# A decoder's latent attention loop: keys turned by a transposing transfer instead of TensorE, rows rotated by VectorE two batches ahead, contexts formed a batch later

## The chip, the cores and the metric

The kernel runs on one core of one Trainium2 chip. The metric is the device time of one execution in microseconds (us), taken as the median of several runs. TensorE (PE) multiplies matrices, VectorE (DVE) and ScalarE (ACT) work on rows of SBUF and PSUM, GpSimd (POOL) does a part of the elementwise work, and SyncE (SP) issues the transfers that 16 DMA engines carry out.

## The reference, cut to what matters

The whole program is a two-layer decoder on x of shape (32, 56, 256): in each layer a self attention, a cross attention to a context, and a mixture of experts. The change is in the cross attention of layer 0, the latent attention. Its context is (32, 1500, 64): 32 batches of 1500 rows of 64 numbers.

```python
kv_rope = kv_c * cos[None] + _rotate_half(kv_c) * sin[None]      # (32, 1500, 64)
q_r = jnp.einsum('bshq,hqr->bhsr', q_big, W_qr)
k_r = jnp.einsum('bld,hdr->bhlr', kv_rope, W_kr)
scores = jnp.einsum('bhsr,bhlr->bhsl', q_r, k_r)
attn = jax.nn.softmax(scores, axis=-1)
ctx_c = jnp.einsum('bhsl,bld->bhsd', attn, kv_rope)
```

The rotated rows serve twice: turned (64 on partitions, rows along the free axis) as keys for the scores, and as they are as values for the contexts.

## The kernel before

The latent attention (function `latent_attention`) first makes the queries of all 32 batches (`QT`), multiplied with the products of all weights, so that the scores of one batch are one product of 16 heads x 56 queries against 1500 rows. Then comes the loop over the 32 batches, the subject of the change. Every engine has an order written out by hand in its own `body(b, par)`; `over_tiles` runs the first two batches unrolled, the middle ones two by two in a hardware loop and the last ones unrolled, and `par` is the buffer, b mod 2. Semaphores alone tie the engines.

One batch has 1500 rows as 12 tiles (KT) of 125 rows (KP). Its work:

- SP loads the rows of the batch after (`lat_raw`, L2454), copies the queries of a batch into both halves of the partitions (`lat_Q`, four transfers, L2471), and takes the denominators of two batches back through DRAM: `spread_reciprocals` sends `lat_den` to 128 partitions (L2482), waits for the reciprocals, stores them (L2486) and loads them spread over the partitions (`lat_rD`, L2493).
- POOL rotates the rows in fp32 with four operations on 125x768 or 125x384 (L2520, L2522, L2525, L2528), ACT rounds them to fp16 (`high`, L2696), and POOL subtracts that from the exact rows to get the low halves (L2534). High and low halves lie side by side in `kk`. ACT also copies the rotated rows to `kv` (L2702).
- PE turns `kk`: 12 tiles, each in two halves of 64 columns, in two portions of 8 and 4 tiles (`turn`, L2582), into PSUM bank 7; ACT copies each portion to `kT` (`evacuate`, L2687). Each batch has a portion of 8 tiles, done a batch ahead, and one of 4.
- PE computes the scores in three groups `g` of four units (L2617; a unit is 8 heads x 2 tiles, three terms of high and low halves), ACT takes the exponential of each unit (L2739) into `Pb`, which has 8 slots. The ring of score banks holds three units, so the fourth unit of a group waits for the exponential of the first.
- After the scores of a group PE multiplies four tiles of `Pb` with `kv` (`values`, L2595, fp32). The last four tiles of a batch come in group 0 of the next.
- DVE sums the 12 tiles of `Pb` in 11 additions (`lat_dsum`, L2819 and L2824), each dependent on the one before. After these sums are complete PE multiplies them with ones (`denominators`, L2605, group 0 of the next batch). ACT copies the context (L2708) and the denominators (L2714) out of PSUM, DVE takes reciprocals (L2805, after the addition of tile 6) and multiplies context and reciprocals (`context`, L2809, after the addition of tile 10).

The lines that make POOL wait for a free buffer, and PE for the low halves:

```python
                        if past(b, 2):
                            pool.wait_ge(kT_done, (b - 1) * NTURN)
                        nc.gpsimd.tensor_tensor(halves(par, True), paired(rot[:, par]),
                                                halves(par, False), ALU.subtract).then_inc(kl_made, 1)
```

## Time and profile before

| | us |
|---|---|
| median of 3 runs | 1811.01 |
| lowest and highest of the 3 | 1799.75, 1813.59 |
| the profiled execution | 1797.95 |
| its span | 1796.2 |
| the loop over batches in it, first scores to last denominators | 354.4 to 961.6 |
| one batch in the steady part of the loop | 18.73 |

| engine | busy us | share of the span |
|---|---|---|
| PE | 1431.9 | 80% |
| DVE | 1361.9 | 76% |
| ACT | 1053.4 | 59% |
| POOL | 652.1 | 36% |

The profiled execution is quicker than the median of the three timed runs by 13 us. The loop is a third of the span. Busy shares over the whole span mix stages with different limits; what matters for the change are the stretches inside the loop.

### The profile page before, as it was taken

To read this page: it belongs to the slowest core of one execution; us is meant where nothing else is said; L and a number is where in the kernel's file an instruction comes from. 1 tells how busy PE (TensorE), PEld (TensorE's weight loads), DVE (VectorE), ACT (ScalarE), POOL (GpSimd) and SP (SyncE) were. 2 spreads that over 40 slices of the span, in tenths; PEclk is the share of its full clock that TensorE was granted. 3 is DMA by queue.
4 is the path that set the end of the run, shared out by engine and by line. 5 is a ranking of instruction groups with operands and counts; after the bars stand their busy time and mean duration, and the time that the engine had idled before them with its cause. 6 is when DMAs were issued, how large, how long until landed. Compare 5 with 4: busy or idle time off the path is not lost. (4 is left out here: it accounts for less than half of the span.)

```text
span 1796.2 us, 40092 instructions
## 1 busy us (share of the span) xinstructions
PE 1431.9 (80%) x13869; PEld 917.4 (51%) x13884; DVE 1361.9 (76%) x2397; ACT 1053.4 (59%) x1795; POOL 652.1 (36%) x658
## 2 busy tenths in 40 slices
PE   1687776899999999999997754992778699945992
PEld 0455553444444444444444743991566567634891
DVE  6888875699988888889886784547898656576774
ACT  1767763577677777777773243551676555454461
POOL 1212213165455465554630145562333200037241
PEclk9856665999999999999998857996899989968996
DMA  6950000111221212222110225444000000034335
GB/s 138 315 165 1 1 1 35 38 36 49 61 59 49 72 48 60 60 48 72 48 45 7 60 74 161 157 148 128 1 1 0 1 2 1 1 96 141 107 102 164
DMA packets 106444, 123.65 MB, mean 69 GB/s; under 512 B 23553, under 2 KB 87625, under 8 KB 106211
## 3 DMA queue, kind: packets, MB, share of 16 engines
q1 hardware_dynamic: 96451, 98.87, 20.5%
q0 software_dynamic: 7776, 21.28, 3.2%
q10 hardware_dynamic: 2112, 2.10, 0.4%
q8 instruction: 66, 1.08, 0.3%
q14 instruction: 39, 0.32, 0.1%
HBM read 66.85 MB, written 40.30 MB: 60 GB/s over the span
## 5 line engine op out<-in xcount | busy, mean ns | idle before, releaser
L2824 DVE TENSOR_TENSOR lat_dsum<-lat_dsum,lat_Pb 125x896 f32<-125x896 f32 x320 | 477.3, 1492 | 67.4 <-ACT lat_Pb L2739 58.5
L2739 ACT ACTIVATE lat_Pb<-banks 125x896 f32<-125x896 f32 x384 | 329.0, 927 | 141.2 <-PE banks L2617 114.8
L2595 PE MATMUL banks<-lat_Pb,lat_kv 125*64 125x448 f32 x1536 | 306.4, 541 | 0.0
L2617 PE MATMUL banks<-lat_Q,lat_kT 64*125 64x448 f16 x2304 | 258.8, 360 | 4.2 <-DVE lat_QT L2785 1.3
L2617 PEld LDWEIGHTS banks<-lat_Q,lat_kT 64*125 64x125 f16 x2304 | 142.6, 134 | 149.3 <-issue 66.9
L2595 PEld LDWEIGHTS banks<-lat_Pb,lat_kv 125*64 125x64 f32 x1536 | 100.6, 137 | 146.4 <-issue 137.6
L2534 POOL TENSOR_TENSOR lat_kk<-lat_rot,lat_kk 125x768 f16<-125x768 f32 x32 | 65.8, 2057 | 279.3 <-ACT lat_kk L2696 279.3
L3165 POOL DMA_INDIRECT sent_outputs<-moe_yb,moe_yidx x98 | 95.6, 975 | 115.5 <-ACT moe_yb L3424 100.5
L3303 PE MATMUL banks<-moe_w2d,moe_gT 88*128 (+3 forms) x780 | 100.0, 278 | 17.6 <-DVE moe_gT L3642 13.7
L3630 DVE COPY moe_xTb<-banks 128x1024 f16<-128x1024 f16 x49 | 33.9, 691 | 76.8 <-PE banks L3270 76.8
L3303 PEld LDWEIGHTS banks<-moe_w2d,moe_gT 88*128 88x128 f16 (+1 forms) x780 | 75.5, 99 | 30.1 <-issue 19.7
L3157 POOL DMA_INDIRECT sent_rows<-moe_arena,moe_idx x64 | 71.2, 1112 | 52.5 <-DVE moe_idx L3571 33.5
L2528 POOL TENSOR_TENSOR lat_rot<-lat_rot 125x768 f32<-125x768 f32 x32 | 80.1, 2502 | 2.5
L3220 PE MATMUL banks<-moe_xTb,moe_w2i 128*88 128x256 f16 (+1 forms) x588 | 73.2, 275 | 0.0
L2520 POOL TENSOR_TENSOR lat_rot<-lat_raw,lat_cosK 125x768 f32<-125x768 f32 x32 | 67.4, 2106 | 14.9 <-POOL lat_kk L2534 9.1
L1471 POOL TENSOR_TENSOR bit_vv<-bit_vf,bit_one 128x256 f16<-128x256 f32 x16 | 11.6, 727 | 164.0 <-PE banks L1758 153.5
L3220 PEld LDWEIGHTS banks<-moe_xTb,moe_w2i 128*88 (+1 forms) x588 | 62.7, 112 | 3.3
L3383 ACT ACTIVATE moe_gT<-banks 88x512 f32<-88x512 f32 x37 | 21.9, 592 | 60.9 <-PE banks L3220 60.9
L3270 PE MATMUL banks<-id,moe_xb 128*128 128x128 f16 x392 | 30.7, 223 | 33.1 <-DMA moe_xb<-sent_rows 33.1
L2522 POOL TENSOR_TENSOR lat_rot<-lat_raw,lat_sinK 125x384 f32<-125x384 f32 x32 | 54.7, 1709 | 2.5
L2525 POOL TENSOR_TENSOR lat_rot<-lat_raw,lat_sinK 125x384 f32<-125x384 f32 x32 | 53.8, 1680 | 2.5
L2687 ACT ACTIVATE lat_kT<-banks 128x1000 f16<-128x1000 f16 x64 | 52.7, 823 | 0.0
(450 smaller groups left out, 3111.8 us busy)
## 6 DMA issues: line engine op xcount, KB each, us to landing
lat_Q<-lat_QT SPq DMA_DIRECT2D x128, 112.0 KB, 3.4
moe_xb<-sent_rows SPq DMA_DIRECT2D x49, 257.0 KB
lat_raw<-in_ctx_dram SPq DMA_DIRECT2D x32, 375.0 KB
sent_rows<-zero SPq DMA_DIRECT2D x1, 7453.0 KB, 39.8
lat_rD<-lat_reciprocals SPq DMA_DIRECT2D x62, 112.0 KB, 2.8
moe_arena<-sent_outputs SPq DMA_DIRECT2D x12, 512.0 KB, 7.5
sent_rows<-zero SPq DMA_DIRECT2D x1, 5140.0 KB, 57.6
sent_outputs<-zero SPq DMA_DIRECT2D x1, 4096.0 KB, 41.6
```

The lines of the kernel that those rows point to most:

```text
L2520: s(nc.gpsimd.tensor_tensor(rot[:, par], r, cosK[:], ALU.mult))
L2522: s(nc.gpsimd.tensor_tensor(rot2[:, :, 0:Q], r[:, :, Q:DC], sinK[:, :, 0:Q], ALU.mult))
L2528: nc.gpsimd.tensor_tensor(rot[:, par], rot[:, par], rot2[:], ALU.add).then_inc(rotated, 1)
L2534: nc.gpsimd.tensor_tensor(halves(par, True), paired(rot[:, par]), halves(par, False), ALU.subtract).then_inc(kl_made, 1)
L2595: ins = nc.tensor.matmul(ps[u * DC:(u + 1) * DC, 6, 0:8 * T], kv[:, par, tt, :], Pb[:, tile_slot(tt, par), u, :], start=tt == 0, stop=tt = ...
L2617: ins = nc.tensor.matmul(ps[0:KP, n % 3 * 2 + q, 0:8 * T], kT[rows, par, 2 * pair + low, 0:KP], Q2[rows, par, w, 8 * u:8 * u + 8, :].rearr ...
L2739: nc.scalar.activation(Pb[:, slot:slot + 2, u, :], ps[0:KP, n % 3 * 2:n % 3 * 2 + 2, 0:8 * T], ACT.Exp, scale=1.0 / QSCALE).then_inc(exp_d ...
L2824: ins = nc.vector.tensor_tensor(dsum[:, par], dsum[:, par], Pb[:, tile_slot(tt, par)], ALU.add)
L3157: nc.gpsimd.indirect_dma_start(xg[:, :], bass.IndirectOffsetOnAxis(ap=idx[:, c, i:i + 1], axis=0), rows[:, i, :], None).then_inc((sent0, s ...
L3165: nc.gpsimd.indirect_dma_start(ytok[:, :], bass.IndirectOffsetOnAxis(ap=yidx[:, n, h:h + 1], axis=0), yb[:, n % 3, h, :], None).then_inc(y ...
L3220: ins = nc.tensor.matmul(ps[0:FP, dst, j * BN:(j + 1) * BN], w[:, u, c, j * FP:(j + 1) * FP], rhs(v, c), start=a + c == 0, stop=a == 2 and ...
L3303: ins = nc.tensor.matmul(dst, gT2[:, n % 2, u, j, h * P:(h + 1) * P], w[:, v, j, :], start=a + j == 0, stop=last and not (gated and b < 0))
```

## The change

What it does, engine by engine:

- **TensorE** no longer turns the keys (24 small matmuls a batch fewer, no `turn`), and **ScalarE** no longer copies them out of PSUM (two activations fewer a batch). `high` of the batch after comes after the third exponential instead of the fourth.
- **SyncE** issues one transposing transfer a batch, `kk` (128 partitions x 12 x 128 fp16, 384 KB) to `kT`, after the low halves of that batch are made. It stands between the copies of the queries and `spread_reciprocals`. PE waits for its landing (`kT_in`) at group 0.
- **GpSimd** rotates the first two batches alone and does nothing in the loop.
- **VectorE** rotates the rows of batch b + 2 after the addition of tile 8 of batch b (four operations), subtracts the low halves of batch b + 1 after tile 2, takes the reciprocals after tile 7 instead of 6, and multiplies the context of batch b - 2 after tile 1, where it multiplied that of b - 1 after tile 10. The copied context has two buffers.
- `kk` is given three more partitions' worth of rows (125 to 128), set to zero once by GpSimd ahead of the loop (32 partitions), and rows of `kT` are 128 long instead of 126. `good` shares the buffer of `den`.

```diff
-            kk = sb("kk", [KP, 2, KT, 2 * DC], F16, c=main)
+            kk = sb("kk", [P, 2, KT, 2 * DC], F16, c=main)
...
-            rD, pv = sb("rD", [P, 8 * T], c=main), sb("pv", [P, 8 * T], c=main)
+            rD, pv = sb("rD", [P, 8 * T], c=main), sb("pv", [P, 2, 8 * T], c=main)
...
+                        sp.wait_ge(kl_made, b + 1)
+                        sp.sem_inc(turn_begun, 1)
+                        sp.dma_start(kT[:, par], kk[:, par].rearrange("p t d -> p (t d)"),
+                                     transpose=True).then_inc(kT_in, 16)
                         if past(b, 2):
                             spread_reciprocals(b - 2)
...
+                    nc.gpsimd.memset(kk[96:P], 0.0).then_inc(rests_zeroed, 1)
...
-                    def turn(b, par, c):
...
-                        for tt in range(8 * c, min(8 * c + 8, KT)):
-                            n = tt - 8 * c
-                            for q in range(2):
-                                rows = slice(q * DC, (q + 1) * DC)
-                                ins = nc.tensor.transpose(
-                                    bank[rows, n * KS:n * KS + KP],
-                                    kk[:, par, tt, rows], id16[0:KP, 0:KP])
-                        ins.then_inc(kT_done, 1)
...
                             if g == 0:
-                                pe.wait_ge(kT_made, b * NTURN + 1)
+                                pe.wait_ge(kT_in, 16 * b + 16)
                                 pe.wait_ge(spread[par], 4 * half_count(b, par))
-                            if g == 2:
-                                pe.wait_ge(kT_made, b * NTURN + 2)
                             for pair in (2 * g, 2 * g + 1):
                                 for u in range(2):
                                     scores(b, par, pair, u)
-                            if g == 0:
-                                turn(b, par, 1)
-                            if g == 2 and live(b + 1, B):
-                                turn(b + 1, (par + 1) % 2, 0)
...
                         if past(b, 2):
-                            act.wait_ge(kT_done, (b - 1) * NTURN)
+                            act.wait_ge(kT_in, 16 * (b - 1))
...
-                            if n == 3:
-                                evacuate(b, par, 1)
-                                if live(b + 1, B):
-                                    high(b + 1, (par + 1) % 2)
+                            if n == 2 and live(b + 1, B):
+                                high(b + 1, (par + 1) % 2)
...
+                    def kept_context(b, par):
+                        dve.wait_ge(pv_kept, b + 1)
+                        dve.wait_ge(rec_in, 32 * b + 32)
+                        context(b, pv[:, par])
+
+                    def rotated_rows(b, par):
+                        r = raw[:, par]
+                        dve.wait_ge(raw_in[par], half_count(b, par))
+                        dve.wait_ge(rotated, b)
+                        dve.wait_ge(kv_made, b - 1)
+                        dve.wait_ge(kl_made, b - 1)
+                        nc.vector.tensor_tensor(rot[:, par], r, cosK[:], ALU.mult
+                                                ).then_inc(products_made, 1)
+                        nc.vector.tensor_tensor(rot2[:, :, 0:Q], r[:, :, Q:DC], sinK[:, :, 0:Q],
+                                                ALU.mult).then_inc(products_made, 1)
+                        nc.vector.tensor_tensor(rot2[:, :, Q:DC], r[:, :, 0:Q], sinK[:, :, Q:DC],
+                                                ALU.mult).then_inc(products_made, 1)
+                        dve.wait_ge(products_made, 3 * b - 3)
+                        nc.vector.tensor_tensor(rot[:, par], rot[:, par], rot2[:], ALU.add
+                                                ).then_inc(rotated, 1)
+
+                    def low(b, par):
+                        dve.wait_ge(kh_made, b + 1)
+                        nc.vector.tensor_tensor(halves(par, True), paired(rot[:, par]),
+                                                halves(par, False), ALU.subtract).then_inc(kl_made, 1)
...
-                            if tt == 6 and past(b, 1):
+                            if tt == 1 and past(b, 2):
+                                kept_context(b - 2, par)
+                            if tt == 2 and past(b, 1) and live(b + 1, B):
+                                low(b + 1, other)
+                            if tt == 7 and past(b, 1):
                                 reciprocals(b - 1)
-                            if tt == KT - 2 and past(b, 1):
-                                dve.wait_ge(pv_kept, b)
-                                dve.wait_ge(rec_in, 32 * b)
-                                context(b - 1, pv[:])
-
-                    over_tiles(dve, body, 0, n=B)
+                            if tt == 8 and live(b + 2, B):
+                                rotated_rows(b + 2, par)
+
+                    over_tiles(dve, body, 1, n=B)
+                    kept_context(B - 2, 0)
```

**SyncE, one batch of the hardware loop.** Before: the queries of the batch, then the denominators and reciprocals of two batches back (ISA and REGISTER_ALU rows work out wait values and addresses).

```order
L2471 DMA lat_Q<-lat_QT 64x2x448
L2471 ISA
L2471 DMA lat_Q<-lat_QT 64x2x448 x3
L2482 DMA lat_den<-lat_den 64x1x7 x2
L2486 ISA
L2486 DMA lat_reciprocals<-lat_rec 128x7
L2489 ISA
L2493 DMA lat_rD<-lat_reciprocals 64x448 x2
```

The same place now:

```order
L2472 DMA lat_Q<-lat_QT 64x2x448
L2472 ISA
L2472 DMA lat_Q<-lat_QT 64x2x448 x3
L2478 DMA_TRANSPOSE lat_kT<-lat_kk 128x12x128
L2487 DMA lat_den<-lat_den 64x1x7 x2
L2491 ISA
L2491 DMA lat_reciprocals<-lat_rec 128x7
L2494 ISA
L2498 DMA lat_rD<-lat_reciprocals 64x448 x2
```

One instruction is new, and the transfers of the denominators, and all behind them, stand behind it and its wait.

**VectorE, the middle of one batch of the hardware loop**, from the reciprocals on. Before:

```order
L2805 RECIPROCAL lat_rec<-lat_den 128x7
L2823 REGISTER_ALU
L2824 TENSOR_TENSOR lat_dsum<-lat_dsum,lat_Pb 125x896
L2814 REGISTER_ALU
L2823 REGISTER_ALU
L2824 TENSOR_TENSOR lat_dsum<-lat_dsum,lat_Pb 125x896
```

Now, with L2760 the reciprocals, L2808 the additions, L2778 to L2785 the rotation of batch b + 2:

```order
L2760 RECIPROCAL lat_rec<-lat_den 128x7
L2798 REGISTER_ALU
L2807 REGISTER_ALU
L2808 TENSOR_TENSOR lat_dsum<-lat_dsum,lat_Pb 125x896
L2774 ISA
L2778 TENSOR_TENSOR lat_rot<-lat_raw,lat_cosK 125x768
L2780 TENSOR_TENSOR lat_rot<-lat_raw,lat_sinK 125x12x32
L2782 TENSOR_TENSOR lat_rot<-lat_raw,lat_sinK 125x12x32
L2784 ISA
L2785 TENSOR_TENSOR lat_rot<-lat_rot 125x768
L2807 REGISTER_ALU
L2808 TENSOR_TENSOR lat_dsum<-lat_dsum,lat_Pb 125x896
```

The four operations of the rotation stand between the additions of tiles 8 and 9, and the beginning of the next batch has the other two that moved:

```order
L2803 TENSOR_TENSOR lat_dsum<-lat_Pb 125x896
L2764 ISA
L2764 TENSOR_TENSOR lat_QT<-lat_pv,lat_rD 128x448
L2798 REGISTER_ALU
L2807 ISA
L2808 TENSOR_TENSOR lat_dsum<-lat_dsum,lat_Pb 125x896
L2789 REGISTER_ALU
L2790 TENSOR_TENSOR lat_kk<-lat_rot,lat_kk 125x6x128
```

There the context (L2764) follows the first addition and the low halves (L2790) the second.

## Rows read from the trace of the kernel before

**Rows 1.** Busy time by stretch: steady loop, stretch, PE, PEld, DVE, ACT, POOL, clock, DMA

```profile
602.99:960.70 357.71, 356.66 (x2816) 161.31 (x2816) 308.33 (x254) 260.68 (x339) 175.95 (x86) 1.00 0.22 54
```

**Rows 2.** Timeline of PE, one batch: start us, us, engine, line, operation

```profile
602.99 2.73 PE L2617 MATMUL banks<-lat_Q,lat_kT 64*125 64x448 f16 x24
605.65 0.41 PE L2582 MATMUL banks<-id,lat_kk 125*64 125x125 f16 x8
605.90 3.18 PE L2595 MATMUL banks<-lat_Pb,lat_kv 125*64 125x448 f32 x16
608.91 0.92 PE L2605 MATMUL banks<-lat_dsum,lat_ones 125*64 125x448 f32 x4
609.75 2.73 PE L2617 MATMUL banks<-lat_Q,lat_kT 64*125 64x448 f16 x24
612.41 3.23 PE L2595 MATMUL banks<-lat_Pb,lat_kv 125*64 125x448 f32 x16
615.57 2.65 PE L2617 MATMUL banks<-lat_Q,lat_kT 64*125 64x448 f16 x24
618.15 0.63 PE L2582 MATMUL banks<-id,lat_kk 125*64 125x125 f16 x16
618.62 3.18 PE L2595 MATMUL banks<-lat_Pb,lat_kv 125*64 125x448 f32 x16
621.72 0.59 PE L2617 MATMUL banks<-lat_Q,lat_kT 64*125 64x448 f16 x4
```

**Rows 3.** Timeline of ACT: denominators copied, once a batch; two long intervals

```profile
378.81 0.54 ACT L2714 ACTIVATE lat_den<-banks 128x448 f32<-128x448 f32 x1
400.81 0.54 ACT L2714 ACTIVATE lat_den<-banks 128x448 f32<-128x448 f32 x1
...
457.68 0.54 ACT L2714 ACTIVATE lat_den<-banks 128x448 f32<-128x448 f32 x1
480.16 0.54 ACT L2714 ACTIVATE lat_den<-banks 128x448 f32<-128x448 f32 x1
```

**Rows 4.** Timeline in the second long interval: DVE, then PE

```profile
473.11 0.62 DVE L2809 TENSOR_TENSOR lat_QT<-lat_pv,lat_rD 128x448 f32 x1 [1.59 <-DMA lat_rD<-lat_reciprocals]
...
476.32 1.53 PE L2605 MATMUL banks<-lat_dsum,lat_ones 125*64 125x448 f32 x4 [2.38 <-DVE lat_dsum L2824]
```

**Rows 5.** Timeline of DVE in the batch of rows 2

```profile
604.90 0.62 DVE L2809 TENSOR_TENSOR lat_QT<-lat_pv,lat_rD 128x448 f32 x1
605.43 1.08 DVE L2824 TENSOR_TENSOR lat_dsum<-lat_dsum,lat_Pb 125x896 f32<-125x896 f32 x1
606.44 1.08 DVE L2819 TENSOR_TENSOR lat_dsum<-lat_Pb 125x896 f32<-125x896 f32 x1
607.56 2.22 DVE L2824 TENSOR_TENSOR lat_dsum<-lat_dsum,lat_Pb 125x896 f32<-125x896 f32 x2
...
617.80 0.19 DVE L2805 RECIPROCAL lat_rec<-lat_den 128x7 f32 x1
617.91 5.97 DVE L2824 TENSOR_TENSOR lat_dsum<-lat_dsum,lat_Pb 125x896 f32<-125x896 f32 x4
```

**Rows 6.** Line L2824, whole program: ns min/median/max, first and last start

```profile
L2824 DVE TENSOR_TENSOR lat_dsum<-lat_dsum,lat_Pb x320: 1083/1093/2661, 358.6 to 958.6; 125x896 f32<-125x896 f32 x160
```

**Rows 7.** Timeline of ACT in the batch of rows 2: groups 0 and 1

```profile
603.97 3.35 ACT L2739 ACTIVATE lat_Pb<-banks 125x896 f32<-125x896 f32 x4 [1.99 <-DVE lat_dsum L2824]
...
611.97 2.54 ACT L2739 ACTIVATE lat_Pb<-banks 125x896 f32<-125x896 f32 x3
```

**Rows 8.** Timeline of SP's queue in that batch: start us, us of issuing

```profile
602.98 2.81 SPq L2471 DMA_DIRECT2D lat_Q<-lat_QT  x4
612.11 1.16 SPq L2482 DMA_DIRECT2D lat_den<-lat_den  x2
...
620.87 0.32 SPq L2454 DMA_DIRECT2D lat_raw<-in_ctx_dram  x1
```

**Rows 9.** Transfers of lat_den, 440 to 640 us: issue to landing

```profile
DMA to landing us min/median/max: 1.8/1.8/1.9
```

More of the change, by code:

```diff
@@ L24 @@
 MAGIC = 12582912.0
-KS = 126
+KS = 128
 KT, KP = 12, 125
@@ L2390, in halves @@
             def halves(par, low):
-                return kk[:, par, low:KT:2, :]
+                return kk[0:KP, par, low:KT:2, :]
             def paired(a):
@@ L2433, in live_columns @@
                 return not isinstance(g, int) or g + 1 < NG
-            own_pool = sem("pool")
+            own_pool, products_made = sem("pool"), sem("row_products_made")
+            Q = DC // 2
             raw_in = [sem("even_rows_loaded"), sem("odd_rows_loaded")]
-            kv_made, kT_done, kT_made = sem("kv_made"), sem("kT_done"), sem("kT_made")
+            kv_made, kT_in = sem("kv_made"), sem("keys_turned")
             rotated, kh_made, kl_made = sem("rows_rotated"), sem("kh_made"), sem("kl_made")
@@ L2443, in latent_attention @@
                 sem("good_reduced"), sem("good_counted"))
-            NTURN = 2
             def past(i, least=0):
@@ L2510, in _ @@
                     pool.wait_ge(tables, 32)
-                    Q = DC // 2
-                    def body(b, par):
-                        r = raw[:, par]
-                        pool.wait_ge(raw_in[par], half_count(b, par))
-                        if past(b, 2):
-                            pool.wait_ge(kv_made, b - 1)
-                        s(nc.gpsimd.tensor_tensor(rot[:, par], r, cosK[:], ALU.mult))
-                        s.settle()
+                    for b in range(2):
+                        r = raw[:, b]
+                        pool.wait_ge(raw_in[b], 16)
+                        if b:
+                            pool.wait_ge(rotated, 1)
+                        s(nc.gpsimd.tensor_tensor(rot[:, b], r, cosK[:], ALU.mult))
                         s(nc.gpsimd.tensor_tensor(rot2[:, :, 0:Q], r[:, :, Q:DC], sinK[:, :, 0:Q],
                                                   ALU.mult))
-                        s.settle()
                         s(nc.gpsimd.tensor_tensor(rot2[:, :, Q:DC], r[:, :, 0:Q], sinK[:, :, Q:DC],
@@ L2527, in body @@
                         s.settle()
-                        nc.gpsimd.tensor_tensor(rot[:, par], rot[:, par], rot2[:],
-                                                ALU.add).then_inc(rotated, 1)
+                        nc.gpsimd.tensor_tensor(rot[:, b], rot[:, b], rot2[:], ALU.add
+                                                ).then_inc(rotated, 1)
                         pool.wait_ge(rotated, b + 1)
                         pool.wait_ge(kh_made, b + 1)
-                        if past(b, 2):
-                            pool.wait_ge(kT_done, (b - 1) * NTURN)
-                        nc.gpsimd.tensor_tensor(halves(par, True), paired(rot[:, par]),
-                                                halves(par, False), ALU.subtract).then_inc(kl_made, 1)
-                        pool.wait_ge(kl_made, b + 1)
-                    over_tiles(pool, body, 0, s, 3, n=B)
+                        nc.gpsimd.tensor_tensor(halves(b, True), paired(rot[:, b]), halves(b, False),
+                                                ALU.subtract).then_inc(kl_made, 1)
                 @block.tensor
@@ L2601, in denominators @@
                         pe.wait_ge(summed, (b + 1) * (KT - 1))
-                        pe.wait_ge(kT_made, min(b + 1, B - 1) * NTURN + 2 if isinstance(b, int)
-                                   else b * NTURN + (NTURN + 2))
+                        if past(b, 1):
+                            pe.wait_ge(den_kept, b)
                         for u in range(2):
@@ L2629, in body @@
                                 queries_of(g)
-                            turn(0, 0, 0)
                             queries_of(NG - 1)
@@ L2680, in keep_queries @@
                                                  ACT.Copy).then_inc(qh_made, 1)
-                    def evacuate(b, par, c):
-                        n = min(8, KT - 8 * c)
-                        act.wait_ge(kT_done, b * NTURN + (c + 1))
-                        if c == 0 and past(b, 2):
-                            act.wait_ge(s_done, (b - 1) * KT)
-                        nc.scalar.activation(
-                            kT[:, par, 8 * c:8 * c + n, 0:KP],
-                            ps[:, 7, :].bitcast(F16)[:, 0:n * KS].rearrange(
-                                "p (n k) -> p n k", n=n)[:, :, 0:KP], ACT.Copy).then_inc(kT_made, 1)
                     def high(b, par):
@@ L2749, in body @@
                                 keep_denominators(b - 1)
-                            if n == 10 and live(b + 1, B):
-                                evacuate(b + 1, (par + 1) % 2, 0)
                     over_tiles(act, body, 1, n=B)
@@ L2810, in context @@
                                                 source, rD[:], ALU.mult).then_inc(ct_made, 1)
+                    def kept_context(b, par):
[16 more added lines that the diff above has]
+                        nc.vector.tensor_tensor(rot[:, par], rot[:, par], rot2[:], ALU.add
+                                                ).then_inc(rotated, 1)
+                    def low(b, par):
+                        dve.wait_ge(kh_made, b + 1)
+                        nc.vector.tensor_tensor(halves(par, True), paired(rot[:, par]),
+                                                halves(par, False), ALU.subtract).then_inc(kl_made, 1)
                     def body(b, par):
+                        if not live(b, B):
+                            return
+                        other = (par + 1) % 2
                         for tt in range(1, KT):
```

24 lines of the change are left out of this document (9 added, 15 removed).

## The prediction

> **What bounds the kernel now.** I first asked for the busy times of the steady part of the loop. TensorE is busy for 356.66 of 357.71 us at full granted clock, VectorE for 308, ScalarE for 261, GpSimd for 176 [rows 1]. A busy PE can still hide waits in the length of its rows, so the timeline of one batch came next [rows 2]: scores start at 602.99 and, a batch later, at 621.72, which is 18.73 us for a batch. In between stand three groups, each of scores and then values. The group in the middle, which has nothing else, takes 2.66 us from its scores to its values (609.75 to 612.41) and 5.82 in all. The turned keys stand in the two others: in the first, values start 2.91 us after the scores, in the third 3.05.
>
> The beginning of the loop is not steady. Denominators are copied once a batch, and two of the intervals are 22.00 and 22.48 us in place of 18.73 [rows 3]. In the second of them VectorE waits 1.59 us for the reciprocals spread by a transfer, and then TensorE waits 2.38 us for VectorE's sum [rows 4]; the row of TensorE is also longer than its like (1.53 against 0.92 [rows 2, 4]).
>
> VectorE has two speeds. An addition lasts 1.08 to 1.12 us in most rows, but four of them take 5.97, 1.49 each [rows 5, 6]. Two facts on its pace: a row followed by an independent one costs less than its duration (the context of 0.62 starts 0.53 before the next, an addition of 1.08 starts 1.01 before), while an addition that waits for the one before costs 1.12 [rows 5].
>
> **The change part by part.**
>
> Turned keys off TensorE. The portion of 4 tiles costs from 605.65 to 605.90, 0.25 us; the portion of 8 from 618.15 to 618.62, 0.47 us [rows 2]. Nothing on TensorE overlaps them, so both are on the path: 0.72 us a batch, a batch of 18.01 us, 31 x 0.72 = 22.3 us in all. The groups then start at 0, 6.51 and 12.33 us of a batch.
>
> Two activations off ScalarE, and the rounding to high halves one unit earlier. ScalarE isn't the bound; what counts is the first exponential of a group, since the fourth unit of scores waits for it. It starts 0.98 us into the group and lasts 0.92 with a pitch of 0.81 (four take 3.35, three 2.54) [rows 7]. The rounding, taken as long as an exponential, then stands before the fourth exponential, which ends at 3.52 + 0.81 + 0.81 = 5.1 us; the first unit of group 1 that needs that exponential's bank comes after 6.5. I cost it at nothing. If it were late, it would add at most its own 0.8 us.
>
> GpSimd out of the loop. The four-in-a-row additions at 1.49 would fall to 1.12. VectorE gets five operations a batch that are new to it. Their durations here come from its own rows: 448 elements take 0.62 and 896 take 1.08 [rows 5], so 1.03 ns an element and 0.16 fixed; 768 elements make 0.95, 384 make 0.56. At 0.08 less for an independent follower, the rotation costs 0.87 + 0.48 + 0.48 + 0.87, and 0.1 for the wait for the products: 2.8 us. The low halves cost 0.87. The sum of VectorE for a batch: 5 additions at 1.01 and 6 at 1.12, 11.8; context 0.53; reciprocals 0.1; rotation and low halves 3.7; together 16.1 us in 18.0. It fits with 1.9 us to spare, but in a fixed order, so the places matter. Walking through a batch: tile 8 can be added when the second exponential of group 2 ends, 12.33 + 0.98 + 0.92 + 0.81 = 15.0 us. Then come the addition, the rotation and three more additions, to 22.2, which is 4.1 us into the next batch. TensorE wants the complete sum for the denominators at 608.91 - 602.99 - 0.25 = 5.7 us into it [rows 2]. That leaves 1.5 us. Then tile 1, the context, tile 2 (whose exponential is there at 5.1) and the low halves, made at 7.6 us. Caught up by tile 4, which has to wait for its exponential to 9.6. So VectorE is late at one place and idle at another, and never holds TensorE.
>
> The stalls at the beginning. Both parts of the cause go: additions beside GpSimd's operations, and a context that waits for its reciprocals in the batch in which they are made. The new place of the context is a batch later, so the transfer has some 4 us more than it needs. I take both long intervals back to normal: 3.27 + 3.75 = 7.0 us.
>
> The transposing transfer. The trace has none, so its cost T (issue on SP, or the time until the rings are free behind it, whichever is more) has to be bounded. What hangs on it is not mainly the keys: low halves at 7.6 us, keys needed at 18.0, so over 10 us for issue and landing. It is what stands behind it in SP's queue, the transfers of the denominators. Before, these are issued at 612.11, 9.1 us into the batch, for 1.16 us, with 1.8 to land [rows 8, 9]. VectorE's reciprocals wait for that landing, and all of VectorE's batch is queued behind the reciprocals, the next low halves too. That closes a ring: low halves, transfer T, denominators (half of the issue and 1.8 of landing, with 0.2 for semaphores: 2.6 us), reciprocals, tile 8, rotation, tiles 9 to 11, tile 1, context, tile 2, low halves: 0.1 + 1.01 + 2.8 + 1.12 + 1.12 + 1.01 + 1.01 + 0.53 + 1.01 + 0.95 = 10.7 us. The ring takes T + 13.3. Up to T = 4.7 it is shorter than TensorE's 18.01 and costs nothing. At 5.4 all of the gain of the steady loop is gone.
>
> Bounds for T: one transfer is issued in 0.32 us at the least; four copies of queries take 2.81, 0.70 each [rows 8]. Each of these has 128 runs of 448 elements, so 5.5 ns a run; the new transfer has 128 x 12 = 1536 rows of 256 bytes, which at that price take 8.4 us. Counting its 12 blocks as 12 transfers gives 12 x 0.32 = 3.8 at the low price and 8.4 at the high. I keep 0.3 and 8.4 as the ends and take 3.8: it is one instruction, as a load is, but cannot be one move. A gain below zero isn't in it.
>
> A rule on this: the Trainium skill, in "DMA: Bandwidth & Descriptors", "Latency and other measured facts", gives 261 GB/s for a transposing transfer on one kernel; for 393,216 bytes that would be an estimated 1.5 us, and the sum would stay as it is. The same page has, for earlier generations, 262,144 cycles of issue for 8,192 tiles, and calls the tile one of 256 bytes in "SDMA does more than copy"; by that reading 1,536 tiles would take an estimated 49,152 cycles, tens of microseconds a batch, and the loop would be more than twice as long. No run here shows either yet; it is a reason not to trust the low end too far.
>
> The rest: zeroing on GpSimd lies ahead of the loop, beside other work; the last context comes after the loop, where VectorE otherwise waits for the last denominators, at most 0.5 us; both at nothing.
>
> **The sum** is 22.3 + 7.0 = 29.3 us. Against the profiled execution, 1797.95, it gives 1769. That execution is 13 us quicker than the median of the three runs; against the median, 1811.01, it gives 1782, and that is my forecast, since the result is a median.
>
> **The rivals.**
>
> *The transfer holds the ring* (slower). Decides from T = 5.4 upward. For it: 1536 short rows, and a queue in which everything waits in turn; against it: a single instruction on idle rings. At T = 7 a batch takes 20.3 us, 31 x 1.5 = 48 more, less the 7 of the beginning: 1852. At 8.4 it takes 21.7, and the time is 1896.
>
> *The transfer takes a part*. T between 4.7 and 5.4, a batch of about 18.4: 10 + 7 gained, 1794.
>
> *VectorE becomes the bound*. If the rotation costs double (the halves of 32 columns are strided, and no row shows them on VectorE), 16.1 becomes 18.9 us, and a batch lasts 18.9: 5 lost, 7 gained, 1809.
>
> *TensorE gets its 0.72 us back as waits*, because the fourth unit of scores or the values then wait for exponentials: the turn would have been cover for ScalarE. Against it: the group without a turn has the same 2.66 us [rows 2]. Only the 7 us stay: 1804.
>
> **How the numbers follow.** Chances: the forecast 0.52, the transfer as the bound 0.22, a part 0.12, waits instead 0.08, VectorE 0.06. A kernel like this can be told from no change from about 1% on, 18 us, so below 1793 is faster and above 1829 slower. Faster: the forecast and a third of the partial case, 0.55. Slower: the transfer above T = 6.1 and a rest for the other cases, 0.20. Within 1%: 0.25. The range: 1764 is 5 below the sum against the profiled execution, for waits that I haven't counted; 1855 is the transfer at T = 7.1. What is left out, mostly a T above that, is 0.15.
>
> **What would show it.** Values 2.6 us after scores in all three groups; the interval between two copies of denominators 18.0 from the second batch on; every addition 1.09; rotation rows of 0.95 and 0.56; on SP a transposing row of under 4.7 us, and the reciprocals not waiting. I am wrong if that row, or the landing of the denominators behind it, is longer; VectorE's reciprocals would then wait each batch, and TensorE before the denominators.

## The result, and the profile after

| | before | changed |
|---|---|---|
| median of 4 runs, us | 1809.5 | 1779.8 |
| lowest and highest | 1799.75, 1813.59 | 1776.0, 1782.12 |
| profiled execution, its span | 1797.95, 1796.2 | 1782.12, 1780.3 |
| mean interval between two copies of denominators | 18.97 | 18.10 |

The ratio of changed to before is 0.9847, with a 95% interval of 0.9811 to 0.9884: 1.5% less time, and clear of the noise. The forecast was 1782.

The copies of the denominators on ScalarE in the changed kernel, the rows that answer to [rows 3]:

```profile
379.91 0.54 ACT L2674 ACTIVATE lat_den<-banks 128x448 f32<-128x448 f32 x1
397.96 0.54 ACT L2674 ACTIVATE lat_den<-banks 128x448 f32<-128x448 f32 x1
416.09 0.54 ACT L2674 ACTIVATE lat_den<-banks 128x448 f32<-128x448 f32 x1
...
887.36 0.54 ACT L2674 ACTIVATE lat_den<-banks 128x448 f32<-128x448 f32 x1
905.17 0.54 ACT L2674 ACTIVATE lat_den<-banks 128x448 f32<-128x448 f32 x1
922.91 0.54 ACT L2674 ACTIVATE lat_den<-banks 128x448 f32<-128x448 f32 x1
```

Read as intervals between their starts, there is no long one any more: 18.05, then 18.13 throughout, and 17.81 and 17.74 for the two last batches, which are written out. TensorE's timeline over one batch, from group 1 to group 0 of the next, against [rows 2]:

```profile
595.55 2.73 PE L2594 MATMUL banks<-lat_Q,lat_kT 64*125 64x448 f16 x24
598.21 3.23 PE L2572 MATMUL banks<-lat_Pb,lat_kv 125*64 125x448 f32 x16
601.37 2.65 PE L2594 MATMUL banks<-lat_Q,lat_kT 64*125 64x448 f16 x24
603.95 3.23 PE L2572 MATMUL banks<-lat_Pb,lat_kv 125*64 125x448 f32 x16
607.11 2.73 PE L2594 MATMUL banks<-lat_Q,lat_kT 64*125 64x448 f16 x24
609.77 3.23 PE L2572 MATMUL banks<-lat_Pb,lat_kv 125*64 125x448 f32 x16
612.83 0.92 PE L2582 MATMUL banks<-lat_dsum,lat_ones 125*64 125x448 f32 x4
613.68 2.73 PE L2594 MATMUL banks<-lat_Q,lat_kT 64*125 64x448 f16 x24
```

Scores to values is 2.66, 2.58 and 2.66 us in the three groups. Values that follow scores directly last 3.16 us to the next scores (603.95 to 607.11); those that followed a turn took 3.10 (618.62 to 621.72 in [rows 2]), and in group 0, to the denominators, 3.06 now and 3.01 before. VectorE in the same stretch, with L2808 the additions, L2790 the low halves, L2778 to L2785 the rotation:

```profile
594.59 1.08 DVE L2808 TENSOR_TENSOR lat_dsum<-lat_dsum,lat_Pb 125x896 f32<-125x896 f32 x1
595.59 0.95 DVE L2790 TENSOR_TENSOR lat_kk<-lat_rot,lat_kk 125x768 f16<-125x768 f32 x1
596.46 1.08 DVE L2808 TENSOR_TENSOR lat_dsum<-lat_dsum,lat_Pb 125x896 f32<-125x896 f32 x1
598.81 4.47 DVE L2808 TENSOR_TENSOR lat_dsum<-lat_dsum,lat_Pb 125x896 f32<-125x896 f32 x4 [1.27 <-ACT lat_Pb L2698]
603.20 0.19 DVE L2760 RECIPROCAL lat_rec<-lat_den 128x7 f32 x1
604.12 1.09 DVE L2808 TENSOR_TENSOR lat_dsum<-lat_dsum,lat_Pb 125x896 f32<-125x896 f32 x1 [0.72 <-ACT lat_Pb L2698]
605.12 0.95 DVE L2778 TENSOR_TENSOR lat_rot<-lat_raw,lat_cosK 125x768 f32<-125x768 f32 x1
605.99 0.55 DVE L2780 TENSOR_TENSOR lat_rot<-lat_raw,lat_sinK 125x384 f32<-125x384 f32 x1
606.46 0.55 DVE L2782 TENSOR_TENSOR lat_rot<-lat_raw,lat_sinK 125x384 f32<-125x384 f32 x1
607.05 0.96 DVE L2785 TENSOR_TENSOR lat_rot<-lat_rot 125x768 f32<-125x768 f32 x1
607.92 3.33 DVE L2808 TENSOR_TENSOR lat_dsum<-lat_dsum,lat_Pb 125x896 f32<-125x896 f32 x3
```

Additions that follow each other have a pitch of 1.12 (4.47 for four), and VectorE is idle at two places a batch, 1.27 and 0.72 us, both times until an exponential is done. SP's queue there, against [rows 8]:

```profile
596.63 1.49 SPq L2478 DMA_TRANSPOSE lat_kT<-lat_kk  x1
598.16 1.51 SPq L2487 DMA_DIRECT2D lat_den<-lat_den  x2
603.52 0.38 SPq L2491 DMA_DIRECT2D lat_reciprocals<-lat_rec  x1
```

The transposing transfer is issued in 1.49 us. Its time from the start of issue to landing, over the stretch from 440 to 900 us:

```profile
DMA to landing us min/median/max: 3.7/3.7/3.7
```

**Where the time went.** Between the first and the last copy of denominators lie 569.24 us before and 543.00 now, 26.2 less. Of these, the beginning gives 7.9 (its four intervals of 22.00, 19.40, 22.48 and 18.98 less four of 18.73) and 30 intervals of 0.61 less give 18.3. The medians are 29.7 apart. The two profiled executions are only 15.8 apart: behind the last copy of denominators the changed one needed 857.4 us and the one before 848.1, in code that is the same, apart from the last context. In the 150 us from 438 us behind the loop's end, for instance, the granted clock was 0.87 against 0.94. That is a difference between two executions. No run separates it from the change, and I don't ascribe it to the change: in the second measurement of the changed kernel, beside the one before, the medians are 25.6 us apart, close to the 26.2 of the loop.

### The profile page after: what moved, and what is told of

Its sections match the earlier page's. It is cut to its first block and busy times, and to the rows that moved or that the text cites. A ratio compares the mean times of both kernels' runs of the same rounds, so it can differ in the third digit from the quotient of the medians.

```text
span 1780.3 us, 38229 instructions
## 1 busy us (share of the span) xinstructions
PE 1423.0 (80%) x13101; PEld 909.2 (51%) x13116; DVE 1342.5 (75%) x2547; ACT 1009.8 (57%) x1731; POOL 349.8 (20%) x509
## 5 line engine op out<-in xcount | busy, mean ns | idle before, releaser
L2808 DVE TENSOR_TENSOR lat_dsum<-lat_dsum,lat_Pb 125x896 f32<-125x896 f32 x320 | 349.5, 1092 | 70.1 <-ACT lat_Pb L2698 62.5
L3290 PEld LDWEIGHTS banks<-moe_w2d,moe_gT 88*128 88x128 f16 (+1 forms) x780 | 77.0, 101 | 30.9 <-issue 19.2
L3386 ACT ACTIVATE moe_uT<-banks,moe_bug 128x256 f32<-128x256 f32 x56 | 23.5, 471 | 49.7 <-PE banks L3207 44.9
L2870 PE MATMUL banks<-lat_B,lat_C 128*56 128x256 f16 x768 | 43.9, 279 | 8.3 <-DVE lat_C L2898 8.3
L2558 PE MATMUL banks<-lat_cols,lat_A 128*128 (+1 forms) x192 | 40.3, 361 | 9.5 <-DVE lat_cols L2726 9.5
L2870 PEld LDWEIGHTS banks<-lat_B,lat_C 128*56 128x56 f16 x768 | 43.4, 110 | 8.5 <-issue 8.3
L3629 DVE TENSOR_TENSOR moe_gT<-moe_gT 88x512 f16<-88x512 f32 (+1 forms) x65 | 44.6, 688 | 3.9 <-ACT moe_gT L3374 2.9
L1131 DVE TENSOR_REDUCE causal_mx<-banks 128x16 f32<-128x896 f32 x16 | 17.5, 1092 | 37.5 <-PE banks L853 37.5
```

The lines of the kernel that those rows point to most:

```text
L2558: ins = nc.tensor.matmul(ps[:, j % 4, 0:GN], A16[:, w, c, 2 * j:2 * j + 2, :].rearrange("p h d -> p (h d)"), cols[:, v, c, ds(g * GN, GN)] ...
L2808: ins = nc.vector.tensor_tensor(dsum[:, par], dsum[:, par], Pb[:, tile_slot(tt, par)], ALU.add)
L2870: ins = nc.tensor.matmul(ps[u * HALF:u * HALF + T, s4 % 2, 0:D], C16[:, s4, low, u, j * T:(j + 1) * T], B16[:, j, wlow, :], start=j == 0 a ...
L3290: ins = nc.tensor.matmul(dst, gT2[:, n % 2, u, j, h * P:(h + 1) * P], w[:, v, j, :], start=a + j == 0, stop=last and not (gated and b < 0))
L3629: nc.vector.tensor_tensor(gT2[:, n % 2, 1], gT[:, n % 2], gT2[:, n % 2, 0], ALU.subtract).then_inc(gl_made, 1)
```

## The experiments

Ten more measurements were made, each of one kernel beside the kernel before on the same chip. The kernel before has medians from 1809.5 to 1828.8 us in these groups, up to 19 us apart, so the ratios count, and the interval between copies of denominators in each trace. That interval hardly varies: the changed kernel has the same 18.10 in the traces of both of its measurements.

| kernel | ratio to before (95%) | mean interval, us | steady interval, us |
|---|---|---|---|
| changed | 0.9847 (0.9811 to 0.9884) | 18.10 | 18.13 |
| turns kept beside the transfer | 0.9967 (0.9946 to 0.9988) | 18.71 | 18.73 |
| rotation alone | 0.9960 (0.9938 to 0.9982) | 18.71 | 18.73 |
| transfer alone | 1.0043 (1.0023 to 1.0064) | 19.10 | 18.13, with long ones |
| transfer twice | 1.0020 (1.0003 to 1.0037) | 19.09 | 19.03 to 19.13 |
| context early | 0.9873 (0.9826 to 0.9920) | 18.10 | 18.13 |
| a value tile between the scores | 0.9898 (0.9863 to 0.9933) | 18.35 | 18.35 |
| transfer and late context | 0.9933 (0.9902 to 0.9964) | 18.50 | 18.47 to 18.72 |
| low halves later | 1.0053 (1.0034 to 1.0073) | 19.22 | 19.25 |
| all batches written out | 0.9789 (0.9741 to 0.9836) | 17.74 | 17.74 |
| changed, again | 0.9849 (0.9801 to 0.9896) | 18.10 | 18.13 |

**Was it TensorE's time?** The changed kernel with transposes of a constant tile at the old places; nobody reads them:

```diff
+                        for tt in range(8 * c, min(8 * c + 8, KT)):
...
+                                nc.tensor.transpose(bank[rows, n * KS:n * KS + KP],
+                                                    id16[0:KP, rows], id16[0:KP, 0:KP])
...
+                            if g == 0:
+                                stand_in(1)
+                            if g == 2 and live(b + 1, B):
+                                if past(b, 1):
+                                    pe.wait_ge(den_kept, b)
+                                stand_in(0)
```

> The changed kernel, with TensorE issuing the same 24 small transposes a batch at the old places (8 after the scores of group 0, 16 after those of group 2), of a constant tile into bank 7, where nobody reads them; the keys still come by the transfer. Theory (the 0.72 us a batch were TensorE's time): the interval between copies of denominators goes from 18.13 back by 0.7 to 18.8 us, the time to about 1780 + 22 = 1802. Rival (TensorE was waiting for something else, and the turns only filled that wait): the interval stays at 18.1 to 18.3 and the time below 1786.

The interval is 18.73, the very one of before, and the ratio loses 0.012 of the changed kernel's gain of 0.015. TensorE's timeline of this kernel has the turns' pitch of 0.25 and 0.47 us again:

```profile
610.02 2.65 PE L2605 MATMUL banks<-lat_Q,lat_kT 64*125 64x448 f16 x24
612.60 0.63 PE L2572 MATMUL banks<-id 125*64 125x125 f16 x16
613.07 3.18 PE L2583 MATMUL banks<-lat_Pb,lat_kv 125*64 125x448 f32 x16
616.17 2.73 PE L2605 MATMUL banks<-lat_Q,lat_kT 64*125 64x448 f16 x24
618.83 0.41 PE L2572 MATMUL banks<-id 125*64 125x125 f16 x8
619.08 3.18 PE L2583 MATMUL banks<-lat_Pb,lat_kv 125*64 125x448 f32 x16
```

These transposes wait for no keys, and their cost is the same. So the turns were TensorE's own time, without any cover, and the rest of the change does nothing for the steady interval while they are there.

**The rotation alone.** The changed kernel with `turn` and `evacuate` back and no transfer:

```diff
-                        sp.wait_ge(kl_made, b + 1)
-                        sp.sem_inc(turn_begun, 1)
-                        sp.dma_start(kT[:, par], kk[:, par].rearrange("p t d -> p (t d)"),
-                                     transpose=True).then_inc(kT_in, 16)
...
+                            if g == 0:
+                                turn(b, par, 1)
+                            if g == 2 and live(b + 1, B):
+                                turn(b + 1, (par + 1) % 2, 0)
```

> The changed kernel without the transposing transfer: TensorE turns the keys and ScalarE copies them out as before, while VectorE rotates the rows, the low halves are early and the contexts a batch later. Theory (the rotation's part of the change is worth only the two long intervals at the loop's start): steady interval 18.7 to 18.85 us, no interval over 19 at the start, time about 1810 - 7 = 1803. Rival (moving the rotation off GpSimd speeds up each batch): steady interval 18.4 or less, time 1795 or less.

The steady interval is 18.73, the first 18.66, and none is long. It gains 0.4%, the stalls of the beginning, and nothing else. This kernel has ScalarE's two copies of the turned keys again, which the one with constant transposes lacks, at the same 18.73: they cost the loop nothing.

**The transfer alone.** The kernel before, with the transfer for the turns; GpSimd and the contexts as they were:

```diff
+                        sp.wait_ge(kl_made, b + 1)
+                        sp.sem_inc(turn_begun, 1)
+                        sp.dma_start(kT[:, par], kk[:, par].rearrange("p t d -> p (t d)"),
+                                     transpose=True).then_inc(kT_in, 16)
...
-                            pool.wait_ge(kT_done, (b - 1) * NTURN)
+                            pool.wait_ge(kT_in, 16 * (b - 1))
```

> The kernel before with the transposing transfer in place of the turns, and nothing else of the change: GpSimd rotates in every batch, the contexts are where they were. Theory: the steady interval falls to 18.1 us as in the changed kernel, but the long intervals at the start stay, so 1810 - 19 to - 22, about 1790. Rival (with additions slowed beside GpSimd VectorE can't keep 18.1 us, so the rotation had to move for the transfer to pay): steady interval 18.4 or more, or new waits of TensorE for VectorE's sum; time 1797 or more.

The rival held. Most intervals are 18.13 as in the theory, but every second to fifth one is 20.5 to 22.3, through the whole loop, and the sum is slower than before. From the waits from 440 to 900 us (engine, what, for whom: us in total, times, longest):

```profile
ACT lat_Pb L2709 <- DVE lat_dsum L2791: 24.7, 11, 2.5
PEld banks L2593 <- DVE lat_dsum L2791: 23.5, 13, 3.3
DVE lat_QT L2776 <- DMA lat_rD<-lat_reciprocals: 19.5, 19, 1.8
```

VectorE waits for the spread reciprocals (the last row) and is late; TensorE (second row) waits for its complete sum before the denominators, and ScalarE (first row) for an addition that frees a slot of `Pb`.

**Which part of the rest heals that?** First the late context added to the transfer, with GpSimd still rotating:

```diff
-                            if tt == KT - 2 and past(b, 1):
-                                dve.wait_ge(pv_kept, b)
-                                dve.wait_ge(rec_in, 32 * b)
-                                context(b - 1, pv[:])
...
+                            if tt == 1 and past(b, 2):
+                                kept_context(b - 2, par)
```

> The kernel before with the transposing transfer and the contexts a batch later in two buffers; GpSimd still rotates all batches. With the transfer alone half of the intervals were 18.13 us, and every few batches one of 20.5 to 22.3 came, where VectorE had waited for the spread reciprocals. Theory (the additions slowed beside GpSimd make the stalls; the late reciprocals are their consequence): most of the long intervals stay, mean interval 18.6 or more. Rival (the wait of the context was the cause): the long intervals are gone, mean interval 18.3 or less, and the rotation need not have moved.

Between the two: the long intervals are gone, so it took the wait of the context to make them, against my theory; but 18.5 is left in place of 18.13, and the ratio is 0.9933, a gain, where the transfer alone was a loss. The busy times of two batches (stretch, PE, PEld, DVE, ACT, POOL, clock, DMA), and VectorE's groups from 440 to 900 us (count, busy us, mean ns), show what then bounds it:

```profile
564.92:601.90 36.98, 36.56 (x250) 15.57 (x248) 36.43 (x27) 24.93 (x32) 21.11 (x11) 1.00 0.44 80
```

```profile
L2796 DVE TENSOR_TENSOR lat_dsum<-lat_dsum,lat_Pb 125x896 f32<-125x896 f32 x248 | 378.8, 1527 | 6.8
L2791 DVE TENSOR_TENSOR lat_dsum<-lat_Pb 125x896 f32<-125x896 f32 x25 | 63.3, 2532 | 0.0
```

VectorE is busy for 36.43 of 36.98 us. Its additions take 1.53 us in the mean and the first of a batch, which lies beside GpSimd's low halves, 2.53, where 1.09 is the pace of the changed kernel. The mean hides two kinds of addition. The kernel before has them too, and there the row of four additions of 5.97 us [rows 5] comes apart into one of 2.59, which lies across GpSimd's last sum, and three of 1.09 behind it:

```profile
617.01 2.54 POOL L2528 TENSOR_TENSOR lat_rot<-lat_rot 125x768 f32<-125x768 f32 x1
617.91 2.59 DVE L2824 TENSOR_TENSOR lat_dsum<-lat_dsum,lat_Pb 125x896 f32<-125x896 f32 x1
620.54 1.09 DVE L2824 TENSOR_TENSOR lat_dsum<-lat_dsum,lat_Pb 125x896 f32<-125x896 f32 x1
```

An addition that meets no operation of GpSimd takes 1.09 in both kernels. The rotation and low halves on GpSimd so cost VectorE 10 x 0.44 + 1.4 = 5.8 us a batch in this kernel; done by VectorE itself, their rows come to 3.96. Then the context put back in the changed kernel:

```diff
-                            if tt == 1 and past(b, 2):
-                                kept_context(b - 2, par)
...
+                            if tt == KT - 2 and past(b, 1):
+                                kept_context(b - 1, other)
```

> The changed kernel with the context of batch b - 1 after the addition of tile 10 of batch b, as before the change (its two buffers stay). The reciprocals are spread by a transfer issued at about 605.0 to 606.1 of the changed trace and landing 2.8 later, 608.9; the addition of tile 10 ends near 610.2. Theory (with the rotation off GpSimd the old place would do): no waits of VectorE for that transfer, interval 18.13, time within 3 us of the changed kernel. Rival (the later context is what keeps VectorE on time): it waits for the transfer, the interval rises above 18.3.

As the theory says: 18.13 in every interval of the hardware loop and no wait for the transfer. The late context is needed only as long as VectorE is slowed; in the changed kernel it brings nothing that these runs could measure.

**The ring over SP and VectorE.** The transfer twice, one after the other:

```diff
-                        sp.dma_start(kT[:, par], kk[:, par].rearrange("p t d -> p (t d)"),
-                                     transpose=True).then_inc(kT_in, 16)
+                        for n in range(2):
+                            if n:
+                                sp.wait_ge(kT_in, 32 * b + 16 * n)
+                                sp.sem_inc(turn_begun, 1)
+                            sp.dma_start(kT[:, par], kk[:, par].rearrange("p t d -> p (t d)"),
+                                         transpose=True).then_inc(kT_in, 16)
```

> The changed kernel with the transposing transfer done twice a batch, the second after the first has landed, so that the transfers of the denominators stand behind 3.7 + 1.5 = 5.3 us in place of 1.5. Theory of the ring (low halves, transfer, denominators, reciprocals, rotation, sums, low halves; 10.7 us of VectorE and 3.3 of the denominators with their measured issue of 1.51 and landing of 2.3): it takes 5.3 + 14.0 = 19.3 us, the interval rises from 18.13 to 19.2 to 19.5, and VectorE's reciprocals wait each batch; time about 1780 + 36 = 1816. Rival (the queue has slack for it, as only the keys' landing counts, which would be at 7.6 + 7.5 = 15 of 18 us): interval and time unchanged.

The interval is 19.1, just under the 19.2 to 19.5 expected, and the wait is where the ring has it. VectorE, from one low halves' row to the next reciprocals, and the queue:

```profile
614.30 0.95 DVE L2794 TENSOR_TENSOR lat_kk<-lat_rot,lat_kk 125x768 f16<-125x768 f32 x1
615.17 5.59 DVE L2812 TENSOR_TENSOR lat_dsum<-lat_dsum,lat_Pb 125x896 f32<-125x896 f32 x5
623.57 0.20 DVE L2764 RECIPROCAL lat_rec<-lat_den 128x7 f32 x1 [2.81 <-DMA lat_den<-lat_den]
...
615.35 5.23 SPq L2482 DMA_TRANSPOSE lat_kT<-lat_kk  x2
620.63 1.48 SPq L2491 DMA_DIRECT2D lat_den<-lat_den  x2
```

From the low halves' end (615.25) to the reciprocals it is 8.3 us: 5.4 until the issue of the denominators begins and 2.9 from there to the reciprocals. And the low halves three additions later:

```diff
-                            if tt == 2 and past(b, 1) and live(b + 1, B):
+                            if tt == 5 and past(b, 1) and live(b + 1, B):
```

> The changed kernel with the low halves after the addition of tile 5 instead of tile 2. By the ring of the prediction with the measured transfer: 14.0 + 1.5 us plus three more additions, 3.3, makes 18.8 to 18.9 against TensorE's 18.13, so the interval rises to 18.8 to 19.0 and the reciprocals wait; time about 22 us over the changed kernel. Rival (the denominators' transfers have slack): interval stays at 18.13.

The interval is 19.25, over the 18.8 to 19.0 expected. Its reciprocals wait 2.5 us a batch, and inside the ring VectorE also waits 0.55 for an exponential between tiles 3 and 4, which the expectation had left out:

```profile
613.36 2.22 DVE L2808 TENSOR_TENSOR lat_dsum<-lat_dsum,lat_Pb 125x896 f32<-125x896 f32 x2 [0.55 <-ACT lat_Pb L2698]
...
621.04 0.20 DVE L2760 RECIPROCAL lat_rec<-lat_den 128x7 f32 x1 [2.48 <-DMA lat_den<-lat_den]
```

The two measure the ring of the changed kernel: 19.1 - (5.3 - 1.5) = 15.3, and 19.25 - 3 x 1.12 - 0.55 = 15.3. Its parts add up to nearly the same, 15.2: 1.6 us from the end of the low halves to the issue of the denominators (596.54 to 598.16 in the changed kernel), 2.9 to the reciprocals, and the 10.7 of VectorE that the prediction added up. The ring has 2.8 us to spare under 18.13. So the early place of the low halves is a necessary part: three additions later the whole change is a loss. By the ring one or two additions later would still cost nothing; that was not tested.

**A value tile between the scores.** An attempt to go further. The fourth unit of scores waits for a free bank, and a tile of values could fill that wait:

```diff
+                            for n in range(4):
+                                if n == 3:
+                                    value_tile(b, par, g, 4 * g - 4)
+                                scores(b, par, 2 * g + n // 2, n % 2)
+                            for tt in range(4 * g - 3, 4 * g):
+                                value_tile(b, par, g, tt)
```

> The changed kernel with the first tile of values of each group put between the third and fourth unit of scores, so that TensorE has 0.75 us of work while the fourth unit's banks are freed. Theory (three waits of some 0.4 us a batch for the exponential of the group's first unit remain in TensorE's time): the interval falls by 3 x 0.4 from 18.13 to 16.9 to 17.2, the ring over SP and VectorE's 16.1 us of work just allow it, and the time is 30 to 37 us under the changed kernel. Rival (switching TensorE between the two kinds of matmul costs as much as it saves, or VectorE's order does not fit): 18.0 or more, no gain.

The rival held: 18.35, slower than the changed kernel's 18.13. One group of that kernel:

```profile
606.98 1.92 PE L2600 MATMUL banks<-lat_Q,lat_kT 64*125 64x448 f16 x18
608.82 0.97 PE L2572 MATMUL banks<-lat_Pb,lat_kv 125*64 125x448 f32 x4
609.73 0.78 PE L2600 MATMUL banks<-lat_Q,lat_kT 64*125 64x448 f16 x6
610.44 2.48 PE L2572 MATMUL banks<-lat_Pb,lat_kv 125*64 125x448 f32 x12
612.84 1.92 PE L2600 MATMUL banks<-lat_Q,lat_kT 64*125 64x448 f16 x18
```

The group takes 5.86 us against 5.74 to 5.82. Scores and values together are 1.84 + 0.71 + 0.91 + 2.40; three tiles at 0.80 would leave 0.80 for the single one and 0.61 for the unit, so each piece of its own costs 0.1 us more. The wait that was there to be saved was 0.1 to 0.2 us a group (2.58 to 2.66 against four units at 0.61), not the 0.4 expected, and the two pieces eat it. Why a separate piece costs more isn't shown.

**All batches written out.** The unrolled last batches had been quicker in both traces:

```diff
-                    over_tiles(pe, body, 1, n=B)
+                    over_tiles(pe, body, 1, n=B, first=B)
```

This is TensorE's line (and the same for SP, ScalarE and VectorE; `over_tiles` then returns before its loop).

> The changed kernel with all 32 batches of the loop written out on each engine, so that waits are for constants and no addresses are worked out. The last two batches, which are written out already, take 17.81 and 17.74 us in place of 18.13, and the groups' first exponential starts 0.82 us in instead of 0.98. Theory (that difference is the cost of the loop form, on the way from scores to exponential): all intervals 17.75 to 17.85, time about 29 x 0.35 = 10 us under the changed kernel beside it. Rival (fetching some thirteen thousand more instructions, or the last batches being quicker only for having no batch after them): intervals stay at 18.1 or show gaps, no gain or a loss.

> The changed kernel once more, beside the one before and the written-out one on the same chip: ratio to the kernel before 0.981 to 0.989 as in the first measurement, interval 18.13.

Written out, every interval is 17.74; the changed kernel beside it has 18.13 and the ratio 0.9849, as in its first measurement. The medians beside each other are 1784.7 and 1795.5: 10.8 us less, for no change of the work; against the kernel before it is 0.9789. TensorE in the kernel written out:

```profile
610.62 2.58 PE L2596 MATMUL banks<-lat_Q,lat_kT 64*125 64x448 f16 x24
613.12 3.23 PE L2574 MATMUL banks<-lat_Pb,lat_kv 125*64 125x448 f32 x16
```

Scores to values is 2.50 instead of 2.66 us; in the trace the difference sits in the time from a group's scores to its first exponential, 0.82 against 0.98. Which part of the loop form makes it (waits against computed values, addresses, the branch) isn't shown.

## Why the prediction was right, and where it wasn't

The time (1782 forecast, 1779.8 measured) and the mechanism of its two terms stand: turned keys, forecast at 22.3 us, gave 18.3 in the loop; the stalls of the beginning, forecast at 7.0, gave 7.9. That the sum of 29.3 us meets the 29.7 between the medians so closely is in part luck: the traces have 26.2 us in the loop, the second measurement has 25.6 between its medians, and the four runs of each kernel spread over 6 and 14 us.

- *Keys off TensorE*: right in mechanism, and the constant transposes show it. The size was 0.72 us a batch by the pitch of the turns' rows; it is 0.61. The term was mis-sized because removing a turn lengthens the values behind it by 0.05 to 0.06 each, as the two timelines show. That is 3.3 us over the loop; the rest is that 31 batches were counted and the traces have 30 intervals.
- *VectorE's work*: durations of 0.95 and 0.56 from a line through two of its rows, measured 0.95 and 0.55; the sum of 16.1 us of 18.0 a batch, measured 254.9 of 290.0 in 16 batches, 15.9. One row was misread: the four additions of 5.97 us are not 1.49 each but one of 2.59 and three of 1.09, and the other three slow ones of that batch (4.87 us for three, at 613.01) are in none of the rows shown. The sum didn't rest on it, since it took 1.01 and 1.12 for all of them. Group times, the late place (the sum done 1.5 us ahead) and the idle place before tile 4 came as walked through.
- *The transfer*: T of 3.8 was taken between 0.3 and 8.4; it is 1.5 us of issue. The 3.8 came from counting 12 blocks as 12 transfers, which no run bears out; the bounds lay on both sides of the threshold, so that the price fell on the right side was not worked out but guessed. The threshold was put at 4.7; from the two experiments it is 1.5 + 2.8 = 4.3, since issue and landing of the denominators came to 2.9 instead of 2.6 and another 0.1 to 0.2 lies between the transfer and them. The ring exists, and the two tries at lengthening it came to 19.1 and 19.25, so the slower rival had the right mechanism and only its price did not occur. Of the two figures that the prediction took from the Trainium skill, "DMA: Bandwidth & Descriptors" ("Latency and other measured facts", and the cycles under "Why a DMA increments its semaphore by 16 and not by 1"), the estimated 1.5 us of moving has room in the trace (3.7 us from issue to landing, with an issue of 1.49), which doesn't show the moving by itself; an issue of tens of microseconds, by the prediction's own count of tiles, is ruled out.
- *GpSimd out of the loop*: here the working was incomplete. The step counted the rotation at VectorE's side as five operations added and otherwise as worth the two long intervals. Alone, with the turns still there, that is what it is worth, 0.4%. But with the transfer in place it is worth more. With neither it nor the late context the transfer loses 0.4%; with the late context alone it gains 0.7%; with the rotation off GpSimd and the context early it gains 1.3%, which is not to be told from the 1.5% of the whole change. So either part turns the loss into a gain, and only the rotation gives the full 18.13. I had slow additions before me [rows 5] and asked only whether the new VectorE fits in 18.0, not whether the old one would have.
- *The stalls of the beginning*: right that both causes went; but the two are not equal. With the transfer in place, faster additions alone take the stalls away; the context's new place alone takes away the long intervals and leaves VectorE full. For the kernel before, without the transfer, the two weren't tried apart.
- *TensorE gets it back as waits*, *VectorE becomes the bound*: neither happened in the changed kernel. VectorE is the bound in the kernel with the transfer, the late context and GpSimd's rotation, though not for the reason of the rival: it is the additions that are slow there.

## What to carry to other kernels

The parts of a change can be worth little or less than nothing one by one (here 0.4% and -0.4%) and more together (1.5%): price each with the others absent, too, and above all ask for every engine whether it could have kept the new pace as it was. When a merged row gives a mean, look at its single instructions before using the mean as a speed. Where a queue carries a transfer that a later step of the same engine waits for, add up the closed ring (steps, issue, landing) and compare it with the bound: it costs nothing until it is longer, and then all of it. And when rows of unrolled and looped copies of the same work stand in one trace, their difference is a first estimate of what the loop form costs: here 18.13 less 17.74 us, and writing everything out gave just that.

## What the runs showed of the hardware that I had not expected

- A transposing transfer of 384 KB from SBUF to SBUF is issued in 1.49 us as one instruction and has landed 3.7 us after its issue began. The two small transfers behind it took 1.51 us to issue, against 1.16 [rows 8], and landed 2.1 us after issue, against 1.8 [rows 9].
- Here GpSimd's elementwise work cost VectorE more than it relieved it of: 5.8 us a batch in slower additions, with the transfer and the late context, against 3.96 for doing the work itself. An addition of 1.09 us took 1.77 across GpSimd's 125x384 products and 2.59 across its 125x768 sum. GpSimd is slowed too: in the kernel before its 125x384 product took 0.98 us ahead of the loop, while VectorE did nothing for most of it, and 1.73 in the loop.

```profile
307.26 0.98 POOL L2522 TENSOR_TENSOR lat_rot<-lat_raw,lat_sinK 125x384 f32<-125x384 f32 x1
...
613.39 1.73 POOL L2522 TENSOR_TENSOR lat_rot<-lat_raw,lat_sinK 125x384 f32<-125x384 f32 x1
```

- A batch written out takes 17.74 us and the same batch in a hardware loop 18.13, 2% of the loop.
